# A gated-delta-rule layer with its feed-forward on one core: an end of the program with an order of its own, and the last step's residual in another tile

## Chip, core and metric

One core of one Trainium2 chip runs the whole program in one launch. The metric is the device time in microseconds; before the change the median of 3 runs is 1757.72 us (1757.12 to 1758.14).

## What is computed

The input x is [8, 2048, 256]. A recurrence over the 2048 positions of each of 8 x 16 heads (a gated delta rule on 16 x 16 states) is followed by a layer norm with gain and bias, a residual and a second layer norm, and this by a gated feed-forward (256 to 768 to 256) with a residual and a third layer norm:

```python
x_act = tanh(x);  static = einsum('bld,ed->ble', x_act, W)
# per head: S = lam*S; u = beta*(v - S^T k); S += k u^T; o = S^T q
y  = static + o
a  = layernorm(y) * gamma + beta
x1 = layernorm(x + a)
h  = silu(x1 @ Wg^T / 127) * (x1 @ Wu^T / 127)
out = layernorm(x1 + h @ Wd^T / 127)
```

## The kernel before

**Steps.** The positions are cut in 32 steps (`NS`) of 64 positions, for all 8 batches at once: 512 tokens, held as 4 tiles (`NW`) of 128 tokens by 256 features. Each engine has one program, written out step by step, and engines meet only at semaphores. `all_steps` calls one function per engine (`pe_step`, `dve_step`, `act_step`, `pool_step`, `sp_step`) for `s` from `FIRST` = -1 to `LAST` - 1 = 34. In one call a function writes, mixed by hand, pieces of work of different steps: the preparation of the keys of steps s + 1 and s + 2, the recurrence of step s, the attention norm and first residual norm of step s - 1, and the feed-forward of step s - 2. `live(q)` drops the pieces whose step does not exist. The calls with s = 32, 33 and 34 are thus what is left of the same order when the recurrence has ended: the feed-forward of step 30, the norms of step 31, the feed-forward of step 31. This stretch is called the end here.

**The norms of a step q.** `dve_statistics` and `dve_moments` take mean and variance of y, `pool_bias` (z = 1) makes scale and bias of them, `act_attention_norm` applies them, `pool_attention_norm` multiplies by gamma (L879), `dve_attention_norm` adds that to the residual in `res` and sums it (L468). Then `pool_mean`, four `act_variance` (L683; z = 2), `pool_bias` and four `act_first_norm` (L689) make x1. x1 lies in `xr`, the only tile of its kind; the variance pass writes its squares there too. That is why `act_variance` with z = 2 waits until the last norm of the step before has read `xr`:

```python
if z == 2:
    act.wait_ge(SEM["o"], n_of("o", q - 1))
```

**The feed-forward of a step q.** `pe_transpose_x1` transposes x1 (L246), ScalarE (`x1hi`, L703) and VectorE (`x1lo`, L473) split it in two fp16 parts. For each of 6 tiles t of the hidden layer: `pe_gate` and `pe_up` (4 matmuls each, L252), `act_hidden` (silu, L709), `dve_multiply` (L480), `act_multiply` (the high fp16 part `hhi`, L715), `pool_multiply` (the low part `hlo`, L884). `gate` has two buffers, so `act_hidden` of tile t waits for `pool_multiply` of tile t - 2. `pe_down` (L278) multiplies by the down weights in four pieces: tiles 0 to 3, then 4 and 5, for the first two token tiles; then in two pieces for the other two, after `dve_add_ffn` (L486) has emptied `pd`. `dve_add_ffn` adds the residual x1 in `xr` in place. Then `pool_mean`, `act_variance` and `pool_bias` (z = 3) and `act_last_norm` (L695), which writes a buffer of `v`, and `sp_store_out` stores it (L1021). In every step before 31 the order on TensorE is up 0, gate 0, 1, 2, up 1, 2, gate 3, up 3, 4, gate 4, 5, up 5.

Of the kernel before, what the change touches and what calls it, by code (L numbers as in the profile page):

```python
# [12 lines left out]
P = 128  # L13
# [5 lines left out]
NS = L // T  # L19
# [16 lines left out]
def build(nc, x, W, ln_gamma, ln_beta, eta, lam_logit, w_gate, w_up, w_down, out):  # L36
# [8 lines left out]
    with ctx:  # L45
# [120 lines left out]
        FIRST, LAST = -1, NS + 3  # L166
# [74 lines left out]
        def pe_transpose_x1(pe, q, p, half):  # L241
            if half == 0:
                pe.wait_ge(SEM["x1"], n_of("x1", q))
            pe.wait_ge(SEM["si"], n_of("si", q, half - 1))
            for n in range(NW):
                last = pe.transpose(pg[half][:, n * P:(n + 1) * P], xr[:, n, half * P:(half + 1) * P], ident[:, :])  # L246
            last.then_inc(SEM["x1p"], 1)
# [21 lines left out]
        def pe_down(pe, q, p, g, tiles):  # L269
# [10 lines left out]
            if tiles[-1] == NHT - 1:  # L280
                last.then_inc(SEM["dn"], 1)

# [200 lines left out]
        def dve_add_ffn(dve, q, p, n):  # L483
            if n % 2 == 0:
                dve.wait_ge(SEM["dn"], n_of("dn", q, n // 2 + 1))
            dve.scalar_tensor_tensor(xr[:, n, :], pd[:, (n % 2) * D:(n % 2 + 1) * D], W_SCALE / HS, xr[:, n, :],  # L486
                                     ALU.mult, ALU.add, accum_out=sm3[:, n:n + 1]).then_inc(SEM["r2"], 1)

# [197 lines left out]
        def act_first_norm(act, q, p, n):  # L686
            if n == 0:
                act.wait_ge(SEM["nm2"], n_of("nm2", q))
            act.activation(xr[:, n, :], res[:, n, :], ACT.Identity, bias=nm2[:, n:n + 1],  # L689
                           scale=rs2[:, n:n + 1]).then_inc(SEM["x1"], 1)  # L690

        def act_last_norm(act, q, p, n):
            if n == 0:
                act.wait_ge(SEM["nm3"], n_of("nm3", q))
            act.activation(v[:, 1 - p, n, :], xr[:, n, :], ACT.Identity, bias=nm3[:, n:n + 1],  # L695
# [15 lines left out]
        def act_multiply(act, q, p, t):  # L711
# [3 lines left out]
            act.activation(hhi[:, t, :], gate[:, t % 2, :], ACT.Copy).then_inc(SEM["hh"], 1)  # L715

# [165 lines left out]
        def pool_multiply(pool, q, p, t):  # L882
            pool.wait_ge(SEM["hh"], n_of("hh", q, t + 1))
            pool.tensor_tensor(hlo[:, t, :], gate[:, t % 2, :], hhi[:, t, :], ALU.subtract).then_inc(SEM["hl"], 1)  # L884

# [136 lines left out]

        def sp_step(sp, s, p):
# [55 lines left out]
        def _(eng):  # L1079
# [17 lines left out]
            all_steps(eng, sp_step)  # L1097
            eng.wait_ge(SEM["out"], NS * PER["out"])

        @block.gpsimd  # L1100
        def _(eng):
# [21 lines left out]
            all_steps(eng, pool_step)  # L1123

        @block.scalar
        def _(eng):
# [9 lines left out]
            all_steps(eng, act_step)  # L1136

        @block.vector
        def _(eng):
# [47 lines left out]
            all_steps(eng, dve_step)  # L1187

        @block.tensor
        def _(eng):  # L1190
# [18 lines left out]
            all_steps(eng, pe_step)  # L1209

# [22 lines left out]
```

## Time and profile before

| what | value |
|---|---|
| median of 3 runs | 1757.72 us (1757.12 to 1758.14) |
| the profiled execution's own time | 1760.27 us |
| its span, first to last instruction | 1758.5 us |
| busy: TensorE, VectorE, ScalarE, GpSimd | 79%, 80%, 63%, 46% of the span |
| busy from 1700 us on (58.5 us) | 27.5, 11.9, 23.8, 16.7 us |
| mean granted clock of TensorE | 0.855 of full speed |

The span is what the profiler saw between the first and the last instruction; the execution's own time is 1.8 us more. In the profile PE is TensorE, PEld its weight loads, DVE VectorE, ACT ScalarE, POOL GpSimd and SP the engine that issues the DMAs. A row of a timeline names start, length, engine, line, operation, the tile written and the tiles read, and in brackets the idle time of the engine before it with the instruction that ended it. The chain of waits goes back from the last instruction, each time to what released it.

### The profile page before, as it was taken

The numbers are of one execution on the slowest core, as the hardware profiler recorded it, in microseconds if no ns is written. First come the engines' busy times: TensorE is split into PE (matmuls) and PEld (weight loads), VectorE is DVE, ScalarE is ACT, GpSimd is POOL, SyncE is SP. The second block draws the span as 40 slices with busy tenths as digits, with TensorE's granted clock in tenths as the row PEclk, the third lists the DMA queues.
The fourth block names the chain that finished last, engine by engine and source line by source line (L and its number), as shares of the span: only waits on it lengthen the run. The fifth ranks groups of instructions, "written<-read, shape, count | busy, mean of one in ns | idle before, by whom it ended". The sixth has DMA issues, their size and how long they took to land.

```text
span 1758.5 us, 53677 instructions
## 1 busy us (share of the span) xinstructions
PE 1384.7 (79%) x21032; PEld 1077.1 (61%) x21032; DVE 1398.9 (80%) x3461; ACT 1104.1 (63%) x2357; POOL 802.2 (46%) x1106
## 2 busy tenths in 40 slices
PE   4357888897888888888888888888889887888764
PEld 3345666675666666666666676666667666666542
DVE  5578888888888888888888888888888887888741
ACT  3236666666666766676677666667666665676544
POOL 6023454444445544444455444445444443544542
PEclk9568889988888989888889988888998888898777
DMA  4555544555654456555455555654455555445200
GB/s 126 109 102 114 110 115 111 121 106 114 127 120 107 115 119 110 117 115 127 106 120 115 121 106 112 126 106 119 113 124 112 113 114 110 120 110 115 49 25 24
DMA packets 701325, 190.98 MB, mean 109 GB/s; under 512 B 620944, under 2 KB 688528, under 8 KB 701072
## 3 DMA queue, kind: packets, MB, share of 16 engines
q1 hardware_dynamic: 701072, 187.56, 50.1%
q8 instruction: 165, 2.70, 0.7%
q14 instruction: 88, 0.72, 0.2%
HBM read 103.55 MB, written 67.11 MB: 97 GB/s over the span
## 4 chain that ended last, share of the span: by engine, by line
PE 25%; SPq 23%; DVE 21%; DMA 15%; ACT 9%; issue 6%; POOL 1%; ACTq 0%; POOLq 0%; DVEq 0%
PE pc L181 11%; SPq L947 6%; DMA scr_t<-t 6%; SPq L956 6%; SPq L1003 4%; SPq L990 4%; ACT v L683 4%; DMA scr_x<-xt 3%; PE pf L226 3%; PE pf L215 2%; DMA kb<-k 2%; PE pu L252 2%; SPq L1013 2%; DVE S L384 2%; DVE Sp L381 2%
## 5 line engine op out<-in xcount | busy, mean ns | idle before, releaser
L884 POOL TENSOR_TENSOR hlo<-gate,hhi 128x512 f16<-128x512 f32 x192 | 228.7, 1193 | 330.5 <-ACT hhi L715 330.1
L181 PE MATMUL pc<-R,tb 128*128 128x32 f16 x4096 | 158.0, 188 | 130.5 <-DVE R L367 115.7
L181 PEld LDWEIGHTS pc<-R,tb 128*128 128x128 f16 x4096 | 147.5, 118 | 147.6 <-DVE R L367 128.8
L181 PE MATMUL pc<-S,e 128*128 128x32 f16 x4096 | 157.1, 186 | 73.9 <-DVE S L388 73.9
L181 PEld LDWEIGHTS pc<-S,e 128*128 128x128 f16 x4096 | 151.5, 118 | 91.1 <-DVE S L388 83.8
L278 PE MATMUL pd<-wd_t,hhi 128*128 128x256 f16 x768 | 176.1, 276 | 13.9 <-DVE xr L486 8.4
L181 PEld LDWEIGHTS pc<-U,kb 128*128 128x128 f16 x4096 | 155.2, 118 | 44.9 <-DVE U L375 42.7
L215 PEld LDWEIGHTS pf<-xb,e 128*128 128x128 f16 x4096 | 152.4, 118 | 49.5 <-DMA e<-scr_x 31.7
L181 PE MATMUL pc<-U,kb 128*128 128x32 f16 x4096 | 159.6, 190 | 22.0 <-DVE U L375 22.0
L215 PE MATMUL pf<-xb,e 128*128 128x32 f16 x4096 | 156.3, 192 | 25.8 <-DMA e<-scr_x 23.7
L278 PE MATMUL pd<-wd_t,hlo 128*128 128x256 f16 x768 | 175.7, 275 | 0.0
L252 PE MATMUL pu<-x1hi,wu_t 128*128 128x512 f16 x384 | 155.3, 404 | 21.0 <-DVE x1lo L473 12.7
L480 DVE SCALAR_TENSOR_TENSOR gate<-pu,gate 128x512 f32<-128x512 f32 x192 | 130.8, 681 | 50.8 <-ACT gate L709 29.8
L436 DVE TENSOR_TENSOR tt<-tt,gs 128x56 f32<-128x56 f32 (+6 forms) x448 | 157.9, 352 | 15.4
L845 POOL TENSOR_TENSOR bu<-U 128x256 f32<-128x256 f16 x128 | 88.2, 689 | 173.2 <-DVE U L375 172.9
L602 ACT ACTIVATE S<-Sp 128x256 f16<-128x256 f32 x128 | 53.3, 417 | 169.9 <-DVE Sp L381 169.5
L226 PE MATMUL pf<-w_t,xt 128*128 128x256 f16 x1024 | 157.9, 314 | 0.4 <-DVE gs L421 0.4
L431 DVE TENSOR_TENSOR gs<-tt,gh 128x56 f32<-128x56 f32 (+6 forms) x448 | 145.1, 324 | 13.5 <-ACT tt L654 1.1
L252 PE MATMUL pu<-x1lo,wu_t 128*128 128x512 f16 x384 | 154.1, 401 | 0.0
L252 PE MATMUL pg<-x1hi,wg_t 128*128 128x512 f16 x384 | 148.0, 385 | 2.1 <-ACT gate L709 1.5
L252 PE MATMUL pg<-x1lo,wg_t 128*128 128x512 f16 x384 | 146.8, 382 | 0.0
L709 ACT ACTIVATE gate<-pg 128x512 f32<-128x512 f32 x192 | 113.8, 593 | 51.1 <-POOL hlo L884 36.5
(124 smaller groups left out, 3285.7 us busy)
## 6 DMA issues: line engine op xcount, KB each, us to landing
xa<-L_attn_x SPq DMA_DIRECT2D x128, 128.0 KB
scr_x<-xt SPq DMA_DIRECT2D x64, 256.0 KB, 2.2
xb<-scr_x SPq DMA_DIRECT2D x256, 64.0 KB, 2.8
e<-scr_x SPq DMA_DIRECT2D x256, 64.0 KB, 3.7
scr_g<-gs SPq DMA_DIRECT2D x32, 512.0 KB, 3.5
gh<-scr_g SPq DMA_DIRECT2D x32, 512.0 KB, 3.5
kb<-k SPq DMA_DIRECT2D x512, 32.0 KB, 2.2
scr_t<-t SPq DMA_DIRECT2D x64, 256.0 KB, 4.5
```

Source lines behind the costliest of these rows:

```text
L181: last = pe.matmul(pc2[:, :, cols], stationary(h, a), moving[:, :, cols], start=a == 0, stop=a == 1)
L215: last = pe.matmul(pf[n % 2][:, 2 * h * C:2 * (h + 1) * C].rearrange("p (z j) -> p z j", z=2), E[p][:, ez, h, :, :, n].rearrange("p b i -> ...
L226: last = pe.matmul(pf[g][:, (n % 2) * D:(n % 2 + 1) * D], xt[:, half, xz, :, :, n].rearrange("p b i -> p (b i)"), w_t[:, half, wz, :], sta ...
L252: last = pe.matmul(bank[:, :], wt[:, half, t * P:(t + 1) * P], xp[:, half, :], start=half + part == 0, stop=half + part == 2)
L278: last = pe.matmul(pd[:, (n % 2) * D:(n % 2 + 1) * D], hp[:, t, n * P:(n + 1) * P], wd_t[:, t, :], start=n % 2 + t + part == 0, stop=n % 2 ...
L431: dve.tensor_tensor(tmp[:, m, 0:C - 1 - j, :], tt[:, m, j:j + 1, :].to_broadcast([P, j, C - 1 - j, NW]), gh[:, i, j, :][:, None].to_broadc ...
L436: dve.tensor_tensor(tt[:, m, i, :], tt[:, m, i, :], tmp[:, m, 0:C - 1 - j, :], ALU.add)\
L480: dve.scalar_tensor_tensor(gate[:, k, :], pu[k][:, :], W_SCALE * HS / XS, gate[:, k, :], ALU.mult, ALU.mult).then_inc(SEM["h"], 1)
L709: act.activation(gate[:, k, :], pg[k][:, :], ACT.Silu, scale=W_SCALE / XS).then_inc(SEM["si"], 1)
L884: pool.tensor_tensor(hlo[:, t, :], gate[:, t % 2, :], hhi[:, t, :], ALU.subtract).then_inc(SEM["hl"], 1)
L947: sp.dma_start(E[p][DH * b:DH * (b + 1), :, :, b].rearrange("k z h i n -> k (z h) (i n)"), src[:, :, b, :]).then_inc(SEM["e"], 16)
L956: sp.dma_start(xb[DH * b:DH * (b + 1)].rearrange("k z h i n -> k (z h) (i n)"), src[:, :, b, :]).then_inc(SEM["xb"], 16)
```

## The change

1. `LAST` is `NS`, so `all_steps` ends with s = 31, the last call in which a recurrence runs. What the calls with s = 32 to 34 did is written in five functions, `pe_tail`, `dve_tail`, `act_tail`, `pool_tail` and `sp_tail`, in an order of their own. They call the same helpers with the same arguments; no piece is added or left out.
2. A function `x1_of(q)` names the tile of x1: `xa` for step 31, `xr` for all others. `xa` is the tile into which the inputs and keys of a step are loaded (128 x 4 x 256, fp32, as `xr`), and no step after 31 loads any. All readers and writers of x1 go through it.
3. `act_variance` with z = 2 of step 31 waits for the last readers of the keys in `xa` (semaphores `nr` and `k16`) in place of the last norm of step 30. `pool_mean` with z = 3 of step 31 waits for that last norm, since sums, scale and bias of the last norm (`sm3`, `nq3`, `nm3`) still exist once.

```diff
-        FIRST, LAST = -1, NS + 3
+        FIRST, LAST = -1, NS
+
+        def x1_of(q):
+
+            return xa if q == NS - 1 else xr
...
+        def pe_tail(pe):
+            pe_up(pe, NS - 2, 0, 0)
+            pe_gate(pe, NS - 2, 0, 0)
+            pe_gate(pe, NS - 2, 0, 1)
+            pe_up(pe, NS - 2, 0, 1)
...
+            pe_down(pe, NS - 2, 0, 1, range(3, 6))
+            pe_transpose_x1(pe, NS - 1, 1, 0)
+            pe_transpose_x1(pe, NS - 1, 1, 1)
+            pe_gate(pe, NS - 1, 1, 0)
+            pe_up(pe, NS - 1, 1, 0)
+            pe_gate(pe, NS - 1, 1, 1)
+            pe_up(pe, NS - 1, 1, 1)
...
+        def dve_tail(dve):
+            dve_statistics(dve, NS - 1, 1, 2)
+            dve_statistics(dve, NS - 1, 1, 3)
+            dve_moments(dve, NS - 1, 1)
+            dve_multiply(dve, NS - 2, 0, 0)
...
         def act_variance(act, q, p, z, n):
 
-            x_, to, nq, va = ((res, xr, nq2, va2), (xr, v[:, 1 - p], nq3, va3))[z - 2]
+            x_, to, nq, va = ((res, x1_of(q), nq2, va2), (x1_of(q), v[:, 1 - p], nq3, va3))[z - 2]
             if n == 0:
                 act.wait_ge(SEM[f"mq{z}"], n_of(f"mq{z}", q))
-                if z == 2:
+                if z == 2 and q == NS - 1:
+                    act.wait_ge(SEM["nr"], n_of("nr", q))
+                    act.wait_ge(SEM["k16"], n_of("k16", q))
+                elif z == 2:
                     act.wait_ge(SEM["o"], n_of("o", q - 1))
...
             pool.wait_ge(SEM[ready], n_of(ready, q))
+            if z == 3 and q == NS - 1:
+                pool.wait_ge(SEM["o"], n_of("o", q - 1))
...
+        def sp_tail(sp):
+            sp_load_residual(sp, NS - 1, 1)
+            sp_store_out(sp, NS - 2, 0)
+            sp_store_out(sp, NS - 1, 1)
...
             all_steps(eng, pe_step)
+            pe_tail(eng)
```

On VectorE the tail has the two last statistics and the moments of step 31 ahead of all products of step 30, the four residual sums (L468) of step 31 ahead of the last product of step 30, and the rest as before.

On ScalarE, in the end: before the change, from the last attention norms of step 31 (`v<-v,nm,rs`) over the last variance and norm of step 30 (L683, L695) and the first of step 31 (L683, L689) to the feed-forward of step 31:

```order
L669 ACTIVATE v<-v,nm,rs 128x256 x2
L683 ACTIVATE v,va<-xr,nq 128x256 x4
L695 ACTIVATE v<-xr,nm,rs 128x256 x4
L683 ACTIVATE xr,va<-res,nq 128x256 x4
L689 ACTIVATE xr<-res,nm,rs 128x256 x4
L703 ACTIVATE x1hi<-pg 128x512 x2
L709 ACTIVATE gate<-pg 128x512 x2
L715 ACTIVATE hhi<-gate 128x512 x2
L709 ACTIVATE gate<-pg 128x512 x2
```

and now, from the variance of step 31 (L758, now into `xa`), its first norm (L764), the split of x1 (L778), and then pieces of step 30's variance and last norm (L770) among the silus (L784) and high parts (L790) of step 31:

```order
L758 ACTIVATE xa,va<-res,nq 128x256 x4
L764 ACTIVATE xa<-res,nm,rs 128x256 x4
L778 ACTIVATE x1hi<-pg 128x512 x2
L758 ACTIVATE v,va<-xr,nq 128x256 x3
L784 ACTIVATE gate<-pg 128x512
L758 ACTIVATE v,va<-xr,nq 128x256
L784 ACTIVATE gate<-pg 128x512
L790 ACTIVATE hhi<-gate 128x512 x2
L770 ACTIVATE v<-xr,nm,rs 128x256 x2
L784 ACTIVATE gate<-pg 128x512 x2
L790 ACTIVATE hhi<-gate 128x512
L770 ACTIVATE v<-xr,nm,rs 128x256
```

Variance and first norm of step 31 have moved ahead of variance and last norm of step 30, and these into the feed-forward of step 31.

On GpSimd, in the end: before, the low parts `hlo` of step 30 (L884), scale and bias of step 31's attention norm (L869 to L875) and the product with gamma (L879):

```order
L884 TENSOR_TENSOR hlo<-gate,hhi 128x512 x2
L869 TENSOR_TENSOR nm<-mv,minus 128x4
L870 TENSOR_TENSOR rs<-mv,epsq 128x4
L872 TENSOR_TENSOR rs<-rs,mhalf 128x4
L875 TENSOR_TENSOR nm<-nm,rs 128x4
L884 TENSOR_TENSOR hlo<-gate,hhi 128x512 x4
L879 TENSOR_TENSOR v<-v,gamma 128x1024
L859 TENSOR_TENSOR nq<-sm,by_16d 128x4
L860 TENSOR_TENSOR nm<-sm,by_d 128x4
L870 TENSOR_TENSOR rs<-va,eps 128x4
L872 TENSOR_TENSOR rs<-rs,mhalf 128x4
L875 TENSOR_TENSOR nm<-nm,rs 128x4
```

and now, with scale and bias (L1002 to L1008) first, the product with gamma (L1012) behind three of the six low parts (L1017), and the mean of step 31 (L992, L993) ahead of the last two:

```order
L1002 TENSOR_TENSOR nm<-mv,minus 128x4
L1003 TENSOR_TENSOR rs<-mv,epsq 128x4
L1005 TENSOR_TENSOR rs<-rs,mhalf 128x4
L1008 TENSOR_TENSOR nm<-nm,rs 128x4
L1017 TENSOR_TENSOR hlo<-gate,hhi 128x512 x3
L1012 TENSOR_TENSOR v<-v,gamma 128x1024
L1017 TENSOR_TENSOR hlo<-gate,hhi 128x512
L992 TENSOR_TENSOR nq<-sm,by_16d 128x4
L993 TENSOR_TENSOR nm<-sm,by_d 128x4
L1017 TENSOR_TENSOR hlo<-gate,hhi 128x512 x2
L1003 TENSOR_TENSOR rs<-va,eps 128x4
```

The norms of step 31 have moved ahead among the low parts of step 30; three low parts of step 30 stand behind the product with gamma, which stood behind all six.

## Rows read from the trace of the kernel before

**Rows 1.** The page's head.

```profile
span 1758.5 us, 53677 instructions
```

**Rows 2.** The chain that ended last, after 1700 us: start, length, what.

```profile
1715.09 2.08 ACT v L695 x4
...
1717.25 2.08 ACT xr L683 x8
...
1723.19 1.98 PE pg L246 x8
...
1726.57 1.89 PE pu L252 x4
...
1753.34 0.98 ACT v L695 x2
```

**Rows 3.** TensorE's timeline, its end: start, length, line, tiles, idle before.

```profile
1703.77 0.28 PE L278 MATMUL pd<-wd_t,hhi 128*128 128x256 f16 x1 [1.84 <-POOL hlo L884]
...
1705.69 0.28 PE L278 MATMUL pd<-wd_t,hhi 128*128 128x256 f16 x1 [0.87 <-DVE xr L486]
...
1709.87 0.27 PE L278 MATMUL pd<-wd_t,hlo 128*128 128x256 f16 x1
1723.19 1.97 PE L246 MATMUL pg<-ident,xr 128*128 128x128 f32 x8 [13.04 <-ACT xr L689]
...
1730.86 0.38 PE L252 MATMUL pg<-x1hi,wg_t 128*128 128x512 f16 x1
1731.07 0.38 PE L252 MATMUL pg<-x1lo,wg_t 128*128 128x512 f16 x1
```

**Rows 4.** Windows: stretch, its length, busy time of each engine, clock, DMA.

```profile
1726.50:1730.00 3.50, 3.43 (x9) 1.23 (x10) 0.02 (x1) 0.00 (x0) 0.00 (x0) 0.50 0.00 0
1730.00:1742.60 12.60, 10.84 (x58) 5.14 (x56) 4.15 (x6) 6.92 (x12) 6.84 (x6) 1.00 0.00 1
1706.00:1709.50 3.50, 3.50 (x19) 2.46 (x18) 1.47 (x8) 0.00 (x0) 0.02 (x1) 0.52 0.00 0
```

**Rows 5.** Mean durations by line, from 1688.2 us to the end.

```profile
L884 POOL TENSOR_TENSOR hlo<-gate,hhi 128x512 f16<-128x512 f32 x12 | 13.8, 1155 | 22.2 <-ACT hhi L715 22.1
...
L480 DVE SCALAR_TENSOR_TENSOR gate<-pu,gate 128x512 f32<-128x512 f32 x12 | 8.3, 691 | 15.9 <-ACT gate L709 13.5 <-PE pu L252 2.3
L715 ACT ACTIVATE hhi<-gate 128x512 f16<-128x512 f32 x12 | 7.5, 625 | 3.5 <-DVE gate L480 3.5
L709 ACT ACTIVATE gate<-pg 128x512 f32<-128x512 f32 x12 | 7.1, 594 | 9.9 <-PE pg L252 6.5 <-POOL hlo L884 3.3
```

**Rows 6.** VectorE's timeline, same stretch.

```profile
1689.13 0.42 DVE L388 SCALAR_TENSOR_TENSOR S<-S 128x256 f16<-128x256 f32 x1
1689.47 0.42 DVE L455 BATCH_NORM_STATS2 st<-v 128x6 f32<-128x256 f32 x1
...
1706.05 0.42 DVE L468 SCALAR_TENSOR_TENSOR res<-v,res 128x256 f32<-128x256 f32 x1 [0.42 <-POOL v L879]
```

**Rows 7.** GpSimd's timeline, same stretch.

```profile
1692.62 1.16 POOL L884 TENSOR_TENSOR hlo<-gate,hhi 128x512 f16<-128x512 f32 x1 [5.13 <-ACT hhi L715]
1694.65 1.16 POOL L884 TENSOR_TENSOR hlo<-gate,hhi 128x512 f16<-128x512 f32 x1 [0.88 <-ACT hhi L715]
1695.76 0.20 POOL L869 TENSOR_TENSOR nm<-mv,minus 128x4 f32<-128x4 f32 x1
...
1697.51 2.44 POOL L884 TENSOR_TENSOR hlo<-gate,hhi 128x512 f16<-128x512 f32 x2
...
1703.67 2.35 POOL L879 TENSOR_TENSOR v<-v,gamma 128x1024 f32<-128x1024 f32 x1
...
1740.28 2.26 POOL L884 TENSOR_TENSOR hlo<-gate,hhi 128x512 f16<-128x512 f32 x2 [1.28 <-ACT hhi L715]
```

**Rows 8.** VectorE and GpSimd at once, step 31's third window.

```profile
1679.00 0.78 DVE L388 SCALAR_TENSOR_TENSOR S<-S 128x256 f16<-128x256 f32 x1
...
1678.84 0.67 POOL L845 TENSOR_TENSOR bu<-U 128x256 f32<-128x256 f16 x1
```

More of the change, by code:

```diff
@@ L245, in pe_transpose_x1 @@
             for n in range(NW):
-                last = pe.transpose(pg[half][:, n * P:(n + 1) * P], xr[:, n, half * P:(half + 1) * P], ident[:, :])
+                last = pe.transpose(pg[half][:, n * P:(n + 1) * P], x1_of(q)[:, n, half * P:(half + 1) * P], ident[:, :])
             last.then_inc(SEM["x1p"], 1)
@@ L688, in act_first_norm @@
                 act.wait_ge(SEM["nm2"], n_of("nm2", q))
-            act.activation(xr[:, n, :], res[:, n, :], ACT.Identity, bias=nm2[:, n:n + 1],
+            act.activation(x1_of(q)[:, n, :], res[:, n, :], ACT.Identity, bias=nm2[:, n:n + 1],
                            scale=rs2[:, n:n + 1]).then_inc(SEM["x1"], 1)
@@ L715, in act_multiply, with act_tail @@
             act.activation(hhi[:, t, :], gate[:, t % 2, :], ACT.Copy).then_inc(SEM["hh"], 1)
+        def act_tail(act):
+            act_hidden(act, NS - 2, 0, 0)
+            act_hidden(act, NS - 2, 0, 1)
+            act_multiply(act, NS - 2, 0, 0)
+            act_multiply(act, NS - 2, 0, 1)
+            act_hidden(act, NS - 2, 0, 2)
+            act_hidden(act, NS - 2, 0, 3)
+            act_attention_norm(act, NS - 1, 1, 0)
+            act_multiply(act, NS - 2, 0, 2)
+            act_attention_norm(act, NS - 1, 1, 1)
+            act_attention_norm(act, NS - 1, 1, 2)
+            act_attention_norm(act, NS - 1, 1, 3)
+            act_hidden(act, NS - 2, 0, 4)
+            act_multiply(act, NS - 2, 0, 3)
+            act_multiply(act, NS - 2, 0, 4)
+            act_hidden(act, NS - 2, 0, 5)
+            act_multiply(act, NS - 2, 0, 5)
+            act_variance(act, NS - 1, 1, 2, 0)
+            act_variance(act, NS - 1, 1, 2, 1)
+            act_variance(act, NS - 1, 1, 2, 2)
+            act_variance(act, NS - 1, 1, 2, 3)
+            act_first_norm(act, NS - 1, 1, 0)
+            act_first_norm(act, NS - 1, 1, 1)
+            act_first_norm(act, NS - 1, 1, 2)
+            act_first_norm(act, NS - 1, 1, 3)
+            act_transpose_x1(act, NS - 1, 1, 0)
+            act_transpose_x1(act, NS - 1, 1, 1)
+            act_variance(act, NS - 2, 0, 3, 0)
+            act_variance(act, NS - 2, 0, 3, 1)
+            act_variance(act, NS - 2, 0, 3, 2)
+            act_hidden(act, NS - 1, 1, 0)
+            act_variance(act, NS - 2, 0, 3, 3)
+            act_hidden(act, NS - 1, 1, 1)
+            act_multiply(act, NS - 1, 1, 0)
+            act_multiply(act, NS - 1, 1, 1)
+            act_last_norm(act, NS - 2, 0, 0)
+            act_last_norm(act, NS - 2, 0, 1)
+            act_hidden(act, NS - 1, 1, 2)
+            act_hidden(act, NS - 1, 1, 3)
+            act_multiply(act, NS - 1, 1, 2)
+            act_last_norm(act, NS - 2, 0, 2)
+            act_multiply(act, NS - 1, 1, 3)
+            act_hidden(act, NS - 1, 1, 4)
+            act_hidden(act, NS - 1, 1, 5)
+            act_multiply(act, NS - 1, 1, 4)
+            act_multiply(act, NS - 1, 1, 5)
+            act_last_norm(act, NS - 2, 0, 3)
+            act_variance(act, NS - 1, 1, 3, 0)
+            act_variance(act, NS - 1, 1, 3, 1)
+            act_variance(act, NS - 1, 1, 3, 2)
+            act_variance(act, NS - 1, 1, 3, 3)
+            act_last_norm(act, NS - 1, 1, 0)
+            act_last_norm(act, NS - 1, 1, 1)
+            act_last_norm(act, NS - 1, 1, 2)
+            act_last_norm(act, NS - 1, 1, 3)
@@ L1136, in _ @@
             all_steps(eng, act_step)
+            act_tail(eng)
         @block.vector
```

87 lines of the change are left out of this document (85 added, 2 removed).

## The prediction

> **What bounds the kernel now.** The page's first number is the span, 1758.5 us [rows 1]. The slices after it show all engines busy until the recurrence ends and thin after; the change touches only that last part, so I read the chain of waits from 1700 us on. It ends in the last norm of step 31, whose last two instructions end at 1754.32 [rows 2]; issue and landing of the last store fill the 4.2 us to the end of the span. Going back, the chain is serial: step 30's last norm (from 1715.09), step 31's variance (from 1717.25), its transposes (1723.19), its feed-forward (1726.57) [rows 2]. The timeline of TensorE gives the size of it: between the last down matmul of step 30 and the transposes of step 31 it stands idle for 13.04 us, released by the last write of x1 [rows 3]. Nothing else of step 31 can start, as x1 waits for `xr`. The windows show the clock: two stretches of 3.5 us at about half of full speed, 1.2 of 2.4 GHz, one in the down matmuls of step 30, one at the start of step 31's feed-forward, and full speed for the rest of that [rows 4]. Last, GpSimd's and VectorE's timelines give what stands in the way of an earlier x1 [rows 6, 7].
>
> **What moves, part by part.** All times below are on the clock of the profiled execution.
>
> *Statistics and bias first.* Both statistics of step 31 and the moments now stand ahead of all products. VectorE is free for them at 1689.47 [rows 6]; two of 0.35 us and the short moments end near 1690.7. GpSimd's scale and bias took 1695.76 to 1697.51 between low parts, 1.75 us [rows 7], and now end near 1692.5. The first low part starts at 1692.62 [rows 7], so this costs nothing; if it slipped, that low part would slip by as much.
>
> *The products of step 30.* up 1 stands fourth on TensorE, not fifth: a group is four matmuls 0.216 us apart [rows 3], 0.87 us. That is the gap of 0.88 us ahead of the second low part [rows 7], which now follows the first and ends near 1694.9. up 2 stands seventh, not sixth, and ends near 1694.9; product, high part behind one attention norm: low part 2 from about 1696.6 to 1697.8. The attention norms, 0.5 us apart on ScalarE, end near 1698.2. Then gamma, 2.35 us [rows 7], to 1700.5, and only then low part 3, 1.16 us [rows 5], to 1701.7. Before, gamma stood behind all low parts. The four residual sums, 0.42 us long and 0.35 apart, ran with GpSimd idle, released by gamma [rows 6]; now they are free at 1700.5, together with low part 3. Both read SBUF. Here a row decides: an instruction of VectorE with two SBUF inputs, 0.42 us alone [rows 6], took 0.78 us when it started 0.16 us into one of GpSimd, which it outlasted by 0.27 us [rows 8]. So I let the sums run behind low part 3, 1701.7 to 1703.2, product 5 (0.69) and high part 5 (0.62) [rows 5] behind them to 1704.5, mean and low parts 4 and 5 on GpSimd from 1703.3 to 1705.85. Before, they ended where gamma began, 1703.67 [rows 7]: **2.1 us later**. If the sums ran beside low part 3, the silu of tile 5 behind that low part decides, and it is 1705.0, 1.3 us later; if gamma came on top in full, 2.35. I take 2.1, the case the row is nearest to.
>
> The Trainium skill's page "SBUF — State Buffer", section "Who interferes with whom", says the same as an exclusive lock: a VectorE instruction with two SBUF inputs and a GpSimd instruction that reads SBUF exclude each other for a whole instruction. By it 2.1 us would be the term and 1.3 us excluded; it speaks against this order, which puts the two side by side.
>
> *Is x1 there in time?* Step 31's variance now stands behind high part 5, 1704.5. From variance to transposes it took 1717.25 to 1723.19, 5.9 us [rows 2]: x1 is ready at 1710.4. The down matmuls from tile 4 on took 1703.77 to 1709.98 [rows 3], 6.2 us with the slow stretch in it, 4.5 without. From 1705.9 they end at 1712.1 or 1710.4. Either way TensorE does not wait for x1, though at full clock with nothing to spare. **The idle 13.04 us goes**; what is late next is the down matmuls themselves.
>
> *The feed-forward of step 31.* It took 1726.57 to 1742.54 [rows 2, 7]. Its order is now gate 0, up 0, gate 1, up 1, so product 1 waits for 16 matmuls, not 20: 0.87 us less. Among its silus and high parts now stand step 30's last variance and four last norms, 0.52 us each (2.08 for four [rows 2]), and on GpSimd step 30's scale and bias ahead of the first low part. ScalarE waited there before. The two norms ahead of the silu of tile 2 are the only ones that find it ready; a shift of the chain by hand gives back half, 0.43 us. **0.44 us less**; the bounds are 0.87 us less and, with all five pieces on the path (2.6), 1.7 us more.
>
> *After it.* Down, last sums, mean, variance, last norm: 1742.54 to 1754.32, 11.8 us, the same instructions in the same order. The new wait of `pool_mean` for step 30's last norm costs nothing: that norm ends by 1728, the mean is due after 1733. So do the store of step 30, some 6 us ahead of the next one on SP's queue, and the load of the residual, which keeps its place. The waits for the keys' last readers are long met.
>
> *The clock.* A stretch of 3.5 us at half speed costs 1.7 us [rows 4], and both lie on the chain. The new order still leaves TensorE waiting in step 30's down part, longer than before (from the last up group, near 1699.2, to low part 3), so I keep that stretch. The second one followed 13 us of idleness; now only 1.4 us (split of x1) lie between transposes and feed-forward. I take it as gone: 1.7 us less. Bounds: both gone, 3.4 less; a third one, 1.7 more.
>
> **The sum:** -13.0 + 2.1 - 0.4 - 1.7 = **-13.0 us**. From the profiled span of 1758.5 that gives 1745.5; that execution took 1760.3 us, so 1747.3; from the median, 2.6 us lower than it, 1757.7 - 13.0 = **1744.7 us**, 0.74% less. Best ends together: -13.0 + 1.3 - 0.9 - 3.4 = -16.0 (1741.7). Worst: -13.0 + 2.35 + 1.7 + 1.7 = -7.3 (1750.4).
>
> **The rivals.** *A, the clock never falls.* Activity of TensorE is denser than before from step 30's down part on. For it: in the feed-forward it stays at full speed through its waits [rows 4]. Against it: the fall at about 1706, after idle pieces of only 1.84 and 0.87 us [rows 3], and the new gap is longer. It gives 1.7 us more, -14.7: 1743.0.
>
> The Trainium skill's page "TensorE: Matmul & The Clock Gate", section "What's actually happening", has the clock low after idleness and high after sustained work. By it the second slow stretch goes, and the first, which began inside a busy piece, would need the waits ahead of it; it does not exclude A.
>
> *B, the queues give it back.* Step 30's last norm moves into step 31's loop on two in-order engines: `act_last_norm` waits for GpSimd's scale and bias, which waits for a variance piece that stands behind a silu. If these hold the loop, its term is +1.7 in place of -0.4, and the bias adds 1.6 ahead of the first low part: -13.0 + 3.7 = -9.3, 1748.4. Against it: GpSimd idles ahead of each pair of low parts, 1.28 us before the last [rows 7].
>
> *C, the change doesn't do what it says.* If something else holds x1 of step 31 (the residual's load, keys still read in `xa`), the idle time stays and only orders change: 1757, within 0.2%. The readers of the keys belong to the recurrence's preparation, long over; this is improbable.
>
> *D, slower.* TensorE at 1.2 GHz from step 30's down part to the end. Step 31 has 48 matmuls 0.216 us apart and 48 of half that, 15.6 us, and step 30's down part 4.5: 20.1 us more than at full speed, if GpSimd covers none. Without any slow stretch the sum is -14.7, so it ends at +5.4, 1763.1; it decides once over 14.7 of the 20.1 us are added. Against it: 12.6 us at full speed in the same loop [rows 4].
>
> **How the numbers follow.** Forecast 0.62, A 0.20, B 0.13, C 0.03, D 0.02. A measurement of this kernel can tell about 0.2%, 3.5 us, from no change. Faster by more: forecast, A and B, 0.95; within: C, 0.03; slower: D, 0.02. The range takes in A, the forecast with 2.35 for 2.1 or with a third slow stretch, and B's near edge: 1741.5 to 1748.0.
>
> **What would show it.** TensorE's idle time ahead of the transposes near 0 in place of 13.04 us; low part 5 of step 30 ending about 1705.9; the residual sums (L508 now) behind or beside low part 3, stretched if beside; the feed-forward of step 31 taking 13.8 us at full clock; the last 11.8 us unchanged. Up to s = 31 all rows should lie as before. I am wrong if the transposes still wait for ScalarE by over a microsecond, if the feed-forward takes over 16 us at full speed (B), or if the time of the steps before moves.

## The result, and the profile after

| what | before | after |
|---|---|---|
| median | 1757.42 us (4 runs, 1757.05 to 1758.14) | 1740.74 us (4 runs, 1736.96 to 1744.47) |
| profiled execution's own time | 1760.27 us | 1736.96 us |
| its span | 1758.5 us | 1735.2 us |
| its mean granted clock | 0.855 | 0.861 |
| its end: first feed-forward matmul of step 30 to the end of the last norm | 66.08 us | 52.51 us |

The change is faster: the ratio to the kernel before is 0.9917, with a 95% interval of 0.9894 to 0.9940, so 14.6 us less (10.5 to 18.6). This ratio is the one on record for the two sets of runs; the quotient of the two medians would be 0.9905, or 16.7 us, and in the groups below the two ways of comparing differ by up to 3 us. The last row of the table is the stretch that the change rewrites, and it is the measure used below: the distance, in one profile, from the start of the first matmul of step 30's feed-forward (1688.24 before, 1678.49 after) to the end of the last norm (1754.32, 1731.00). It is 13.57 us shorter. The other 9.75 us by which the two spans differ lie ahead of it, where both programs are the same.

```profile
span 1735.2 us, 53678 instructions
```

The chain that ended last, after 1698 us: start, length, engine, tile and line. It answers to [rows 2].

```profile
1696.84 1.06 PE pd L282 x8
...
1698.76 4.17 PE pd L282 x24
...
1703.41 0.61 ACT x1hi L778
...
1705.38 1.04 PE pg L256 x4
...
1716.95 1.39 POOL hlo L1017 x2
...
1725.12 2.08 ACT v L758 x8
...
1730.02 0.98 ACT v L770 x2
```

In [rows 2] the chain ran through step 30's last norm on ScalarE before it could enter step 31. Now it goes from step 30's down matmuls (24 of them from 1698.76) by way of the transposes straight into the feed-forward of step 31. A variance and a last norm stand at its very end only, as before.

TensorE's timeline, with the idle time ahead of a row in brackets; it answers to [rows 3].

```profile
1696.84 0.28 PE L282 MATMUL pd<-wd_t,hhi 128*128 128x256 f16 x1 [2.05 <-POOL hlo L1017]
...
1698.76 0.39 PE L282 MATMUL pd<-wd_t,hhi 128*128 128x256 f16 x1 [0.87 <-DVE xr L526]
...
1702.66 0.27 PE L282 MATMUL pd<-wd_t,hlo 128*128 128x256 f16 x1
1702.77 1.04 PE L250 MATMUL pg<-ident,xa 128*128 128x128 f32 x8
1705.38 0.39 PE L256 MATMUL pg<-x1hi,wg_t 128*128 128x512 f16 x1 [1.58 <-DVE x1lo L513]
...
1712.72 0.39 PE L256 MATMUL pu<-x1hi,wu_t 128*128 128x512 f16 x1 [0.25 <-DVE gate L520]
```

The 13.04 us of idle time ahead of the transposes are gone: they start at 1702.77, 0.11 us after the last down matmul. And the eight transposes take 1.04 us where [rows 3] have 1.97.

Windows: stretch, its length, busy time of PE, PEld, DVE, ACT and POOL, then the granted clock; they answer to [rows 4].

```profile
1678.40:1681.20 2.80, 2.71 (x7) 1.04 (x8) 2.38 (x10) 0.42 (x1) 0.17 (x2) 0.51 0.30 104
1698.70:1701.70 3.00, 2.94 (x15) 2.11 (x16) 0.00 (x1) 2.08 (x4) 0.23 (x2) 0.51 0.00 0
1705.20:1719.00 13.80, 12.46 (x64) 6.08 (x64) 4.27 (x7) 10.11 (x22) 8.03 (x9) 1.00 0.10 30
```

There are two stretches at half speed, 1.2 of 2.4 GHz. The one in step 30's down matmuls stands where it stood before. The one at the start of step 31's feed-forward is gone, the whole loop has a clock of 1.00. The other is at the start of step 30's feed-forward. It is no new stretch but the tail of one that began in the recurrence: the granted clock is 0.50 from 1657.2 to 1681.1 us, in which TensorE was busy for 13.15 of 23.90 us. The profile before has the same, from 1665.2 to 1689.0; there less than 1 us of it falls into the end (0.57 from 1688.2 to 1689.2).

ScalarE, one of step 30's four last norms (line 770) inside the loop of step 31, ahead of a high part (790) that follows without a gap:

```profile
1713.23 0.59 ACT L770 ACTIVATE v<-xr,nm,rs 128x256 f32<-128x256 f32 x1
1713.72 0.61 ACT L790 ACTIVATE hhi<-gate 128x512 f16<-128x512 f32 x1
```

VectorE, two of step 31's four residual sums (line 508 is 468 before); they answer to the last of [rows 6].

```profile
1691.74 1.36 DVE L508 SCALAR_TENSOR_TENSOR res<-v,res 128x256 f32<-128x256 f32 x1 [1.26 <-POOL v L1012]
...
1693.03 0.41 DVE L508 SCALAR_TENSOR_TENSOR res<-v,res 128x256 f32<-128x256 f32 x1
```

The first sum took 1.36 us, the others 0.41. It was released at 1691.74, 0.08 us after GpSimd had begun low part 3, and ended 0.29 us after that low part.

GpSimd, low parts (line 1017), gamma (1012) and the mean of step 31 (992); they answer to [rows 7].

```profile
1683.78 2.33 POOL L1017 TENSOR_TENSOR hlo<-gate,hhi 128x512 f16<-128x512 f32 x2 [0.95 <-ACT hhi L790]
1687.88 1.15 POOL L1017 TENSOR_TENSOR hlo<-gate,hhi 128x512 f16<-128x512 f32 x1 [1.77 <-ACT hhi L790]
1689.35 2.35 POOL L1012 TENSOR_TENSOR v<-v,gamma 128x1024 f32<-128x1024 f32 x1 [0.32 <-ACT v L741]
1691.66 1.15 POOL L1017 TENSOR_TENSOR hlo<-gate,hhi 128x512 f16<-128x512 f32 x1
1694.22 0.20 POOL L992 TENSOR_TENSOR nq<-sm,by_16d 128x4 f32<-128x4 f32 x1 [1.41 <-DVE res L508]
...
1694.52 2.26 POOL L1017 TENSOR_TENSOR hlo<-gate,hhi 128x512 f16<-128x512 f32 x2
...
1716.95 2.27 POOL L1017 TENSOR_TENSOR hlo<-gate,hhi 128x512 f16<-128x512 f32 x2 [1.28 <-ACT hhi L790]
```

Low part 5 of step 30 ends at 1696.78, that of step 31 at 1719.22. Means by line agree with [rows 5]: a low part takes 1155 ns in both. What changed is the idle time ahead of the twelve, 22.2 us before and 5.9 now:

```profile
L1017 POOL TENSOR_TENSOR hlo<-gate,hhi 128x512 f16<-128x512 f32 x12 | 13.7, 1155 | 5.9 <-ACT hhi L790 5.7
```

With these rows the end can be cut at four points and set beside the prediction's terms:

| piece | before | after | difference | predicted |
|---|---|---|---|---|
| first matmul to low part 5 of step 30 | 15.47 | 18.29 | +2.8 | +2.1 |
| from there to the transposes | 19.48 | 5.99 | -13.5 | -13.0 |
| transposes to step 31's first matmul | 3.38 | 2.61 | -0.8 | 0 |
| feed-forward of step 31 to its low part 5 | 15.97 | 13.84 | -2.1 | -0.4 - 1.7 |
| from there to the end of the last norm | 11.78 | 11.78 | 0.0 | 0 |
| sum | 66.08 | 52.51 | -13.57 | -13.0 |

Two things were open. Does the end alone carry the difference, or do the 9.75 us ahead of it belong to the change? And which of its parts does what?

### The profile page after: what moved, and what is told of

It reads as the page before. It is cut to its first block, busy times and chain, and to the rows that moved or that the text cites. A ratio compares the mean times of both kernels' runs of the same rounds, so it can differ in the third digit from the quotient of the medians.

```text
span 1735.2 us, 53678 instructions
## 1 busy us (share of the span) xinstructions
PE 1378.6 (79%) x21032; PEld 1073.9 (62%) x21032; DVE 1397.8 (81%) x3461; ACT 1103.3 (64%) x2357; POOL 803.9 (46%) x1106
## 4 chain that ended last, share of the span: by engine, by line
PE 32%; DVE 23%; SPq 16%; DMA 11%; ACT 10%; issue 6%; POOL 1%; ACTq 0%; POOLq 0%; DVEq 0%
PE pc L185 12%; PE pu L256 4%; DMA scr_t<-t 4%; SPq L1121 4%; SPq L1112 4%; PE pf L219 4%; ACT v L758 4%; PE pg L256 3%; PE pf L230 3%; SPq L1155 3%; SPq L1168 3%; DMA scr_x<-xt 2%; DVE S L424 2%; DVE Sp L421 2%; PE pd L282 2%
## 5 line engine op out<-in xcount | busy, mean ns | idle before, releaser
L1017 POOL TENSOR_TENSOR hlo<-gate,hhi 128x512 f16<-128x512 f32 x192 | 228.9, 1195 | 310.6 <-ACT hhi L790 310.3
L471 DVE TENSOR_TENSOR gs<-tt,gh 128x56 f32<-128x56 f32 (+6 forms) x448 | 145.1, 324 | 13.5 <-ACT tt L726 1.1
L784 ACT ACTIVATE gate<-pg 128x512 f32<-128x512 f32 x192 | 113.8, 593 | 50.8 <-POOL hlo L1017 38.3
```

The source lines that it names most:

```text
L471: dve.tensor_tensor(tmp[:, m, 0:C - 1 - j, :], tt[:, m, j:j + 1, :].to_broadcast([P, j, C - 1 - j, NW]), gh[:, i, j, :][:, None].to_broadc ...
L784: act.activation(gate[:, k, :], pg[k][:, :], ACT.Silu, scale=W_SCALE / XS).then_inc(SEM["si"], 1)
```

## The experiments

Ten experiments ran, on eight different kernels and in three groups, each group beside runs of the kernel before on its own chip: medians of before 1756.14 us (26 runs), 1755.07 us (11 runs) and 1755.3 us (11 runs), with single runs from 1749 to 1766 us. So only ratios within a group are compared.

### The change again

No edit.

> The changed kernel, unchanged. The end is the stretch from the first feed-forward matmul of step 30 to the end of the last norm: 66.1 us in the profile before, 52.5 us in the first profile after, 13.6 less. The span fell by 23.3 us, the median of 4 runs by 16.7. Theory 1 (the edit acts in the end alone; the rest is scatter from run to run of the steps before): the end is again 51 to 54 us; the profiled span minus the end, 1682.6 us in the first profile after and 1692.4 before, lies anywhere from 1680 to 1694, and the difference of the medians over 5 rounds is 12 to 16 us. Theory 2 (the edit also shortens the steps up to 31): span minus end is again near 1683, and the difference of medians is again over 16 us.

Measured: 1745.22 us (1739.42 to 1748.82, 6 runs), ratio 0.9919 (0.9891 to 0.9946). Its end takes 53.28 us, 12.80 less than before, as expected. The difference of the medians, 10.9 us, misses the 12 to 16 that were expected and is far from the rival's "over 16"; the ratio gives 14.2 us. What lies ahead of the end came out as in the kernel before. This is where step 30's product with gamma starts, the last row of GpSimd that the recurrence paces and the change leaves alone; before and after:

```profile
1658.33 2.37 POOL L879 TENSOR_TENSOR v<-v,gamma 128x1024 f32<-128x1024 f32 x1 [0.39 <-ACT v L669]
```

```profile
1648.59 2.39 POOL L1012 TENSOR_TENSOR v<-v,gamma 128x1024 f32<-128x1024 f32 x1 [0.40 <-ACT v L741]
```

and in this second profile of the same program as the latter:

```profile
1657.78 2.38 POOL L1012 TENSOR_TENSOR v<-v,gamma 128x1024 f32<-128x1024 f32 x1 [0.40 <-ACT v L741]
```

The same code has 9.19 us between its two profiles. Over twelve profiles of nine kernels whose instructions are the same up to here, the stretch from the first of these products to this one took 1519.2 to 1530.0 us, before and after anywhere among them. The 9.75 us are scatter of the steps, and the 13.57 us of the end are the change. The half-speed stretch in the down part was some 10 us long here (10.3 at a clock of 0.50), in the first profile of the change 3.4:

```profile
1702.00:1712.70 10.70, 8.51 (x43) 5.51 (x41) 1.86 (x9) 4.67 (x13) 3.97 (x7) 0.52 0.00 0
```

yet the end is only 0.8 us longer, since TensorE waited inside it for GpSimd anyway (from low part 5 to the transposes it took 7.64 us, against 5.99) and step 30's feed-forward started faster.

### The tile alone

The kernel before with `x1_of` and its waits, in the old order of all engines.

```diff
+        def x1_of(q):
+
+            return xa if q == NS - 1 else xr
...
-                if z == 2:
+                if z == 2 and q == NS - 1:
+                    act.wait_ge(SEM["nr"], n_of("nr", q))
+                    act.wait_ge(SEM["k16"], n_of("k16", q))
+                elif z == 2:
```

> The kernel before with x1 of step 31 in the keys' tile and the two changed waits, in the old order. My theory (the order on ScalarE holds step 31's norms behind step 30's, the tile only permits another order): the idle time of TensorE ahead of the last transposes stays 13.0 us, the end 65 to 67 us, the median within 2 us of the kernel before. Rival (the wait for the tile is what holds x1, the engines would sort the rest): idle 5 to 8 us, the end 58 to 61 us. If the time up to the end differs from before by several us with the end unchanged, Theory 1 (scatter, or any edit shifts it) is favoured for the extra gain.

Measured: 1755.89 us (12 runs), ratio 0.9990 (0.9974 to 1.0006), end 65.29 us. TensorE still stands idle ahead of the transposes, now of `xa`:

```profile
1715.00 1.97 PE L250 MATMUL pg<-ident,xa 128*128 128x128 f32 x8 [12.84 <-ACT xa L696]
```

ScalarE works in order, and the variance of step 31 still stands behind step 30's last norm. The tile frees nothing that the order does not use.

### The order without the tile

The change with x1 in `xr`, so step 30's variance and last norm must stand ahead of step 31's on ScalarE, and its last mean and bias ahead of step 31's bias on GpSimd; the orders of the products stay.

```diff
-            return xa if q == NS - 1 else xr
+            return xr
...
             act_multiply(act, NS - 2, 0, 5)
+            act_variance(act, NS - 2, 0, 3, 0)
...
+            act_last_norm(act, NS - 2, 0, 3)
             act_variance(act, NS - 1, 1, 2, 0)
```

> The changed kernel with x1 of step 31 in the old tile, and so with step 30's last variance and norm ahead of step 31's variance on ScalarE, and step 30's last mean and bias ahead of step 31's second bias on GpSimd; all else of the new order kept. My theory (nearly the whole gain is the 13 us of idleness, and the rest of the order alone costs 2 us and gives 0.4): the end 64 to 67 us, TensorE idle 12 to 13 us ahead of the transposes. Rival (the other reorderings carry a good part, 5 us or more): the end 61 us or less.

Measured: 1759.44 us (10 runs), ratio 1.0008 (0.9988 to 1.0028), end 66.56 us.

```profile
1716.97 1.97 PE L250 MATMUL pg<-ident,xr 128*128 128x128 f32 x8 [13.04 <-ACT xr L761]
1720.36 0.61 PE L256 MATMUL pg<-x1hi,wg_t 128*128 128x512 f16 x1 [1.42 <-DVE x1lo L513]
```

The idle time is back to the hundredth, 13.04 us, and with it a feed-forward at half speed for its first part (16.33 us to the end of its low part 5, at a mean clock of 0.83). Everything else in the order is worth nothing by itself that the end (66.56 against 66.08 us) or the ratio shows. Tile and order only pay together.

### The products of step 31 in their old order

```diff
-            pe_gate(pe, NS - 1, 1, 0)
             pe_up(pe, NS - 1, 1, 0)
+            pe_gate(pe, NS - 1, 1, 0)
             pe_gate(pe, NS - 1, 1, 1)
-            pe_up(pe, NS - 1, 1, 1)
             pe_gate(pe, NS - 1, 1, 2)
-            pe_gate(pe, NS - 1, 1, 3)
+            pe_up(pe, NS - 1, 1, 1)
...
```

> The changed kernel with gate and up groups of step 31 on TensorE in the order of before (up 0, gate 0, 1, 2, up 1 ...). My theory (product 1 waits for 20 instead of 16 matmuls, 0.87 us, all of it on the path): the feed-forward of step 31 from its first gate matmul to the last low part 14.7 us at full clock instead of 13.8. Rival (GpSimd and the norms of step 30 in ScalarE's queue set the pace, so nothing changes): 13.8 us.

Measured: 1745.6 us (7 runs), ratio 0.9932 (0.9909 to 0.9956), so the medians do not tell it from the change. The profile does: from the first matmul of the loop (1702.94) to the end of low part 5 (1717.65) 14.71 us, against 13.84. The order is worth 0.87 us, as predicted, the time of four matmuls. It shows as the wait of up 4, the ninth group:

```profile
1702.94 0.39 PE L256 MATMUL pu<-x1hi,wu_t 128*128 128x512 f16 x1 [1.57 <-DVE x1lo L513]
...
1711.13 0.39 PE L256 MATMUL pu<-x1hi,wu_t 128*128 128x512 f16 x1 [1.12 <-DVE gate L520]
```

which has 0.25 us at the same place in the change. This run has the same order of products as the kernel before, but full clock and step 30's norms in the loop; so the two can be compared at the second product of step 31. Before, and here:

```profile
1732.85 0.69 DVE L480 SCALAR_TENSOR_TENSOR gate<-pu,gate 128x512 f32<-128x512 f32 x1 [1.34 <-PE pu L252]
```

```profile
1707.54 0.69 DVE L520 SCALAR_TENSOR_TENSOR gate<-pu,gate 128x512 f32<-128x512 f32 x1 [1.34 <-PE pu L256]
```

From the loop's first matmul to this product it took 6.28 us before and 4.60 here, so the half-speed stretch had cost 1.68 us. From this product to the end of low part 5 it took 9.69 us before and 10.11 here, 0.42 more, with the two norms that stand ahead of the silu of tile 2.

The end of this profile is with 50.95 us shorter than that of the change in spite of the slower loop. Its stretch in the down part was as long as that of the first profile of the change, 3.4 us, but it lay earlier (1691.9 to 1695.3), inside the first down piece and ahead of the end of low part 5 (1695.72), for which TensorE waits in any case: from there to the transposes it took 4.61 us, against 5.99. And step 30's low part 0 came 1.0 us sooner (4.29 us against 5.29). The clock moves one profile's end by more than such an edit.

### The sums beside no low part

The mean of step 31 ahead of low part 3 on GpSimd, so that nothing of GpSimd runs beside the four residual sums. It holds low part 3 back for it.

```diff
             pool_attention_norm(pool, NS - 1, 1)
-            pool_multiply(pool, NS - 2, 0, 3)
             pool_mean(pool, NS - 1, 1, 2)
+            pool_multiply(pool, NS - 2, 0, 3)
             pool_multiply(pool, NS - 2, 0, 4)
```

> The changed kernel with GpSimd's mean of step 31 ahead of low part 3 of step 30, so that no GpSimd instruction runs beside the four residual sums. In the changed kernel the first sum starts 0.08 us into low part 3 and takes 1.36 us where it took 0.42 before. Theory (it waits for the GpSimd instruction): here all four take 0.42 us and start within 0.1 us of the end of gamma. Rival (it is slow for another reason, such as waiting for gamma's writes or for the residual): it takes 1.36 us again. For the time: low part 3 starts 1.7 us later, and from its end to that of low part 5 lie silu, product, high part and low part, 3.3 us, so low part 5 ends 1.1 to 1.3 us later against the start of step 30's feed-forward, and the end grows by 0.7 to 1.3 us: the order of the change, with its blocked sum, is the better one.

Measured: 1739.38 us (one run), end 52.28 us. First VectorE, then GpSimd:

```profile
1693.38 0.43 DVE L508 SCALAR_TENSOR_TENSOR res<-v,res 128x256 f32<-128x256 f32 x1 [1.26 <-POOL v L1012]
...
1694.42 0.42 DVE L508 SCALAR_TENSOR_TENSOR res<-v,res 128x256 f32<-128x256 f32 x1
```

```profile
1685.48 2.27 POOL L1017 TENSOR_TENSOR hlo<-gate,hhi 128x512 f16<-128x512 f32 x2
...
1691.00 2.35 POOL L1012 TENSOR_TENSOR v<-v,gamma 128x1024 f32<-128x1024 f32 x1 [0.32 <-ACT v L741]
1694.93 0.20 POOL L992 TENSOR_TENSOR nq<-sm,by_16d 128x4 f32<-128x4 f32 x1 [1.58 <-DVE res L508]
...
1695.23 2.26 POOL L1017 TENSOR_TENSOR hlo<-gate,hhi 128x512 f16<-128x512 f32 x2
1698.54 1.16 POOL L1017 TENSOR_TENSOR hlo<-gate,hhi 128x512 f16<-128x512 f32 x1 [1.04 <-ACT hhi L790]
```

The first sum takes 0.43 us in place of 1.36, and the fourth starts 1.04 us after it; in the change that is 1.98 us. So the 0.94 us between them were a wait for low part 3 and nothing of the sum's own. This agrees with the Trainium skill's page "SBUF — State Buffer", section "Who interferes with whom": two SBUF inputs on VectorE and a GpSimd instruction that reads SBUF exclude each other for a whole instruction. But taking the block away did not pay: low part 5 ends 14.22 us after the start of low part 0, against 13.00 in the profiles of the change, since low parts 3, 4 and 5 now queue behind the mean. By this piece the change's order is the better one in spite of the block. The whole end did not grow by the 0.7 to 1.3 us that were expected; it is 0.2 us shorter than in the first profile of the change, because low part 0 came 1.0 us sooner and the down part lost less to the clock. One profile and one run show no more than the piece.

### Another order: step 31's split before step 30's last down pieces

Gamma stands behind two low parts, and the transposes ahead of the last two down pieces, whose 24 matmuls then run while ScalarE and VectorE split x1. Step 30's norms stand behind the silus of step 31. The core of it on two engines; VectorE and ScalarE follow, and some gate and up groups of both steps change places too:

```diff
             pe_down(pe, NS - 2, 0, 0, range(4, 6))
-            pe_down(pe, NS - 2, 0, 1, range(0, 3))
-            pe_down(pe, NS - 2, 0, 1, range(3, 6))
             pe_transpose_x1(pe, NS - 1, 1, 0)
             pe_transpose_x1(pe, NS - 1, 1, 1)
+            pe_down(pe, NS - 2, 0, 1, range(0, 3))
+            pe_down(pe, NS - 2, 0, 1, range(3, 6))
...
             pool_multiply(pool, NS - 2, 0, 1)
-            pool_multiply(pool, NS - 2, 0, 2)
             pool_attention_norm(pool, NS - 1, 1)
-            pool_multiply(pool, NS - 2, 0, 3)
             pool_mean(pool, NS - 1, 1, 2)
+            pool_multiply(pool, NS - 2, 0, 2)
+            pool_multiply(pool, NS - 2, 0, 3)
+            pool_bias(pool, NS - 1, 1, 2)
             pool_multiply(pool, NS - 2, 0, 4)
             pool_multiply(pool, NS - 2, 0, 5)
```

> An order of my own for the end. Gamma stands behind low part 1, so x1 of step 31 is due before the last down pieces of step 30; its transposes stand ahead of these two pieces, and its split runs beside them, so the feed-forward of step 31 can start as soon as TensorE is free. Step 30's last variance and norms stand behind most of step 31's silus. By the durations of the rows: x1 ready 4 us earlier than in the changed kernel, the 1.5 us of idleness between transposes and feed-forward gone, the down part 0.7 us shorter in idleness and nothing else; the end 49 to 50.5 us against 52.5 and 53.3 in the two profiles of the changed kernel. Rival (the two in-order queues of ScalarE and GpSimd are full, and what is moved ahead pushes step 30's products back): the end 52 us or more. The median should follow: 2 to 4 us below the changed kernel, hard to see in a scatter of several us.

Measured: 1737.0 us (1734.15 to 1743.51, 6 runs), ratio 0.9898 (0.9872 to 0.9923), end 51.83 us: a miss by 1.3 us against the expected end. Two stretches at a reduced clock account for most of it, one on the transposes and the down pieces behind them, one in the last down part, from the end of low part 5 on 13.44 us in place of 11.78 (the same order, with constant matmuls, took 11.78 in two later profiles):

```profile
1701.90:1703.50 1.60, 1.60 (x13) 1.47 (x11) 1.04 (x5) 0.64 (x2) 0.00 (x0) 0.66 0.00 0
1720.00:1726.00 6.00, 4.25 (x24) 3.03 (x25) 0.78 (x4) 2.07 (x4) 2.19 (x4) 0.74 0.13 38
```

The loop itself took 13.71 us, 0.13 less than in the change. In it step 30's norms no longer stand ahead of a silu that is ready, but its products stand in a different order too (up 2 ahead of gate 2), so this difference is not the price of the norms alone.

### TensorE kept busy in its waits

Constant matmuls into a free tile fill the waits of step 30's down part and of the split. They change no result and cost time only if they outlast the wait.

```diff
+        def pe_filler(pe, count):
+            for _ in range(count):
+                pe.matmul(pc[:, :], wg_t[:, 0, 0:P], wu_t[:, 0, 0:512], start=True, stop=True)
...
+            pe_filler(pe, 9)
             pe_down(pe, NS - 2, 0, 0, range(0, 4))
+            pe_filler(pe, 8)
             pe_down(pe, NS - 2, 0, 0, range(4, 6))
+            pe_filler(pe, 3)
             pe_down(pe, NS - 2, 0, 1, range(0, 3))
...
+            pe_filler(pe, 5)
             pe_gate(pe, NS - 1, 1, 0)
```

> The changed kernel with matmuls of constants into the idle bank of the recurrence, where TensorE waits in the end: 9 behind step 30's last up group, 8 and 3 between its down pieces, 5 behind the transposes of step 31 (each 128x512, 0.216 us apart at full clock, less than the waits they fill). Theory (idleness lets the clock fall; half-speed pieces cost 1.4 us in the first profile after, 3.2 us in the second): no half-speed piece after the first microseconds of step 30's feed-forward, transposes 1.04 us instead of 1.97, the end 51 to 51.5 us. Rival (the clock falls whatever stands in the gaps, or the filler pushes the pieces back): a half-speed piece again, the end 52.5 us or more.

Measured: 1742.52 us (6 runs), ratio 0.9920 (0.9897 to 0.9943), end 50.51 us, half a microsecond less than the 51 to 51.5 that were expected. As expected, no half-speed piece follows the first microseconds, and the transposes take 1.04 us, as they do in the change:

```profile
1682.30:1726.00 43.70, 39.23 (x224) 21.18 (x222) 17.85 (x47) 25.01 (x55) 21.12 (x27) 0.99 0.06 16
```

This is the change's order with the clock all but full from step 30's feed-forward to that of step 31 (0.99; the change has 0.93 from 1678.4 to 1723). By this the change's 52.51 and 53.28 us hold 2.0 and 2.8 us of half speed. In the ratio they do not show: it is that of the change. But its interval reaches 4 us to either side, so a gain of 2 to 3 us could not show in it.

### Both together

The order with the split first, with constant matmuls ahead of the first two down pieces.

```diff
+            pe_filler(pe, 9)
             pe_down(pe, NS - 2, 0, 0, range(0, 4))
+            pe_filler(pe, 8)
             pe_down(pe, NS - 2, 0, 0, range(4, 6))
             pe_transpose_x1(pe, NS - 1, 1, 0)
```

> My order with 9 and 8 such filler matmuls in the two waits for low parts of step 30. If both theories hold, the end is 48 to 49 us, some 4 us less than in the changed kernel, and the median 3 to 5 us less; if the filler costs what it brings, 49 to 50.5 us as without it.

Measured: 1736.81 us (1734.79 to 1743.86, 6 runs), ratio 0.9899 (0.9875 to 0.9923), end 48.31 us.

### The change and this version side by side

Both kernels again, without an edit.

> The change, unchanged, beside the split order on one chip. Theory of scatter (a median of a few runs of one kernel moves by some us because the 31 steps ahead of the end vary from run to run): median ratio to the kernel before 0.990 to 0.994; in the profile the end from the first feed-forward matmul of step 30 takes 50.5 us plus half of the time that TensorE spends at 1.2 GHz in it, so 51.5 to 54; first residual sum 1.3 to 1.4 us; loop of step 31 13.84 and rest 11.78. Rival (the two earlier ratios, 0.9917 and 0.9919, were luck and the change gives the 13 us of the end and nothing else moves): the same 0.992 to 0.994, which differs from 14 us only by 0.001, so the two are told apart only if it comes outside.

> The split order with constant matmuls, again, beside the change on the same chip. If its shorter end counts (48.3 us against 50.5 to 53.3 of the change), its median is 2.2 to 5 us below that of the change, ratio to the kernel before 0.988 to 0.992; end in the profile 48 to 49 us with TensorE at full clock from the first feed-forward matmul on. If the end's length drowns in the scatter of the steps before it, the two medians agree within 1.5 us.

Measured: the change 1740.57 us (6 runs), ratio 0.9926 (0.9901 to 0.9950), end 53.27 us; the other version 1739.33 us (6 runs), ratio 0.9913 (0.9890 to 0.9936), end 48.06 us. The first window is the down part of the change, the second the end of the other version:

```profile
1695.70:1706.10 10.40, 8.21 (x40) 5.22 (x39) 1.60 (x7) 4.67 (x13) 3.97 (x7) 0.51 0.00 0
```

```profile
1682.00:1727.00 45.00, 35.76 (x213) 20.17 (x210) 16.74 (x46) 26.92 (x63) 23.02 (x32) 0.97 0.05 15
```

The ends lie within the expected ranges and are 5.2 us apart. The rule set down for the change, 50.5 us plus half of the time at 1.2 GHz, is too simple: this end has 11.0 us at half speed up to its last matmul, for which the rule gives 56.0 us, measured 53.27; part of that time TensorE waits in any case. The medians are only 1.2 us apart: by the terms set down ahead of it, the shorter end drowned here in the scatter of the steps. Of all comparisons, the split-first order had 0.9898, 0.9899 and 0.9913, the order of the change 0.9917, 0.9919, 0.9926 and 0.9920 (with constant matmuls). Their means are 0.17% apart, 3 us, and every one of the first three is below every one of the others; but each has an interval of 0.0025 to either side. That the end is 4 to 5 us shorter is shown by two profiles, and it has two parts: against the change with constant matmuls (50.51 us) the order gives 2.2 to 2.5 us, the rest is the clock. That the whole program is shorter too, these runs make likely and do not settle. It is faster than the kernel before without doubt.

## Why the prediction was right

**The main term held.** "The idle 13.04 us goes" was the step that carried the prediction, and it went in every profile of the change. Both halves of the edit are needed for it: the tile alone gives 0.9990, the order without the tile 1.0008.

**Step 30's low parts, +2.1 us.** The piece came out 2.8 us longer, but it holds two things. From low part 0 to the end of low part 5 it took 11.09 us before and 13.00 in all three profiles of the change: 1.9 us, and that is the term (its own times, 1705.85 less 1703.67, give 2.2). The row that decided it, a two-input instruction of VectorE beside one of GpSimd [rows 8], said rightly that the sums would wait for low part 3; they did, for 0.94 us. The other 0.9 us are half speed at the start of step 30's feed-forward: the recurrence's half-speed stretch reached 2.6 us into it in the first profile (5.29 us to low part 0), 0.8 us before (4.38) and 0.9 us in the second (4.41).

**x1 in time.** The prediction had x1 ready just as the last down matmul ends at full clock. With the clock kept up by constant matmuls, x1 was ready at 1703.76 and the last down matmul started at 1703.86. In the change itself half speed delayed the matmuls and left 1.5 us to spare, in its two other profiles 3.1.

**The feed-forward of step 31, -0.4 us.** The order's part was sized at 0.87 and measured 0.87. What step 30's norms give back was put at 0.43 and measured 0.42, behind the second product, between the kernel before and the run with the products in their old order. Rival B, which had the loop 1.7 us longer by the queues, is excluded.

**The clock, -1.7 us.** The second stretch went, as predicted, and the loop took 13.84 us for the 13.8 named. Its price in the loop was put at 1.7 and measured 1.68, ahead of the second product. So all three terms of the loop hold one by one, and 0.87 - 0.42 + 1.68 is the 2.13 us by which it is shorter. Not foreseen was that the transposes, too, had run at half speed behind the idle time; at full clock they take 0.93 us less. The stretch in the down part stayed, as predicted, but not with its length: 3.4 us in the first profile, 10.3 and 10.2 in the two others, where low part 5 to the transposes took 7.64 us in place of 5.99. Rival A did not come; constant matmuls show what it would have been worth, an end of 50.51 us, 2.0 to 2.8 us less than the change. The Trainium skill's page "TensorE: Matmul & The Clock Gate", section "What's actually happening", has the clock low after idleness and high after sustained work; the traces agree, with a granted clock of 0.99 with constant matmuls against 0.93 without, and of 0.50 from 1712.9 us, inside the idle 13 us before, to 1730.0; the same transposes took 1.97 us there and 1.04 in the change.

**The size.** The sum was -13.0 us. The end came out 13.57, 12.80 and 12.81 us shorter in three profiles of the change. That these lie so near to it is in part luck: the transposes gave 0.9 us that no term had, and in the last two profiles the longer half-speed stretch took 1.7 us that only the bounds had. The median, 1740.74 us, is 4.0 us below the forecast and 0.8 us below the lower end of the range, 1741.5; by the ratio (14.6 us less) it would be 1742.8, inside. Either is nearer to rival A's 1743.0 than to the forecast, and only the profiles, with their half-speed stretches, exclude A. Of the 4.0 us the end explains 0.6 us at most; the rest is no more than the medians of one kernel moved between groups (1755.07 to 1757.42 us before, 1740.57 to 1745.22 with the change). One sign named ahead was a bad one: "if the time of the steps before moves" would have called the prediction wrong, and it moved by 9 us between two executions of one program.

## What to carry to other kernels

- When an in-order engine releases the wait that ends last, look for both the buffer and the order: a second tile frees nothing while the queue keeps its order, and an order cannot change while one tile serves two steps. An input tile that no later step loads is a second buffer at no cost.
- Measure a change of a short stretch by that stretch, from a fixed instruction to a fixed instruction in each profile. Here 13 us of the end were plain in single profiles, while spans of one program differed by 10.
- Two engines that block each other for one instruction may still be placed side by side: here the block cost 0.94 us, and the one order tried without it took 1.22 us more than the order with it.

## What was not expected

- **The steps' length varies from execution to execution.** From the first to the 31st product with gamma, the same instructions took 1519.2 to 1530.0 us in twelve profiles; single steps took 48.4 to 53.6 us, with a mean of 50.6 to 51.0. Why is open: it was not tried. The first four timed runs of the kernel before lay within 1.1 us and suggested a steadier program than it is; its later runs lay between 1749 and 1766 us.
- **Half-speed stretches of very different length in one program.** In the down part the three profiles of the change have 3.4, 10.3 and 10.2 us of it, with the same order. The first begins in the wait of 0.87 us, 19.7 us after step 30's first matmul, the others 14.5 us after it, inside the first down piece. Why they differ is open.
- **Constant matmuls keep the clock up, and no gain is seen in the whole time.** They took 2 to 3 us off the end, by one profile, and the ratio stayed at 0.9920, with 4 us to either side.
